# An attention block: the low part of the value projection is made on GpSimd from an fp32 copy instead of on VectorE from PSUM

## The chip, the cores and the metric

One core of one Trainium2 chip runs the whole kernel in one launch. The metric is device time in microseconds (us) of that core. One execution was profiled; the others were only timed.

## The reference

```python
x_n = _group_norm(x, gn_w, gn_b)            # x: 4 images of 256 channels, 32 x 32 pixels
q = _conv1x1(x_n, wq, bq)                   # 256 x 256 matrices applied to every pixel
k = _conv1x1(x_n, wk, bk)
v = _conv1x1(x_n, wv, bv)
q, k, v = (to_heads(q), to_heads(k), to_heads(v))      # 4 heads of 64 channels, 1024 pixels
attn = softmax(einsum('bhqd,bhkd->bhqk', q, k) * 64 ** -0.5)
out = _conv1x1(einsum('bhqk,bhkd->bhqd', attn, v), wp, bp)
return x + out
```

Everything is fp32 in the reference.

## The kernel before, in words

Products run on TensorE in fp16 with each factor split in two: the high part is the fp32 value rounded to fp16, the low part is the rest. A product is then three matmuls, high by high, high by low and low by high. So each tensor that a matmul reads has a high and a low tile, and somebody has to make them.

The work is cut into 128 slots, 32 to an image (`TOTAL`, `SLOTS`); G is the slot's number, g its number within the image, U = G // 4 is a unit (a head and half of its queries, 8 to an image), and each slot takes two blocks of 128 keys. Every engine has its own program, an in-order list of what it does slot by slot, written by hand in a function `slot(G)`; semaphores join them.

What happens in slot G:

- TensorE, in this order: the scores of slot G (`scores`, L707 and L708, into PSUM banks `st[G % 2]`); up to two matmuls for the row maxima of a later unit (L652 for one row tile, L678 for a pair of heads); in odd slots the second half of a projection job (L587); the weighing of slot G - 4 (`weigh`, 24 matmuls, L730 to L733, into `pv`), which needs the exponentials of slot G - 4, their low part and the values' low part; a tiny matmul for group statistics in some slots (L635); in even slots the first half of a new projection job.
- ScalarE: the exponentials of slot G twice, as fp16 `p_hi` (L900) and as fp32 `p` (L908, in place in `st` for even G); in odd slots the eviction of the job that has just ended (`job`, L859 to L879); for the next image, the normalised input (L927, L933).
- VectorE: in even slots `low(...)` (L1004) if a value job ended; in odd slots the low part of the exponentials of the even slot before (`p_low`, L1014, in two halves); the row maxima (L990 for a pair, L985 for one), the normalisation of a finished unit (L1021, L1022), statistics of a later image.
- GpSimd: in even slots the split of a key or query job (`high`, L1216, and `low_kq`, L426), the low part of the exponentials of the odd slot before (`p_low`, L1242); residual additions, the split of outputs (L1230, L1232), the low part of the normalised input (L412), and `about_group_mean` (L403 to L407) and `norm_factors` (L1195 to L1203), the small steps from group statistics to the factors of the next image's normalisation.
- SyncE issues nearly all DMAs, in order, among them the row shift that the first scores of a unit need (L467).

A projection job is `(kind, i, j, image)`, with i the half of the channels and j the half of the pixels; its bank is `gen`, one PSUM bank for all. `JOBS` places it: value jobs start at g = 8, 14, 24 and 30 (in the first image also at 2, and one before slot 0), 16 in all. A value job at G is ended by TensorE in slot G + 1, evicted by ScalarE in slot G + 1 and given its low part in slot G + 2. The next job may use `gen` when `bank_empty` says so.

One pair of row maxima in each even slot is put in the scores bank `st[1]`, which the scores of the next, odd slot need. So `scores(G)` in odd slots waits until VectorE has reduced that pair (`in_scores_bank`, `pair_in_bank`, L700).

The lines that make a value tile before:

```python
# ScalarE, L870: high part straight from PSUM
nc.scalar.activation(v_rows(v_hi, i, j), bank..., ACT.Copy, scale=...).then_inc(s_hi["v"], 1)
# VectorE, L1004: low part = scale * PSUM - high part
nc.vector.scalar_tensor_tensor(out=v_rows(v_lo, i, j), in0=gen..., scalar=..., in1=v_rows(v_hi, i, j), ...)
```

`v_rows` is 8 rows of 64 fp16 numbers with a step of 65 in `v_hi` and of 64 in `v_lo`.

The first image has a table of its own for statistics, `FIRST_STATS = {4: ("mean", 1), 6: ("var", 1)}`: in slot 4 GpSimd ends its list with `about_group_mean`, whose result `dev2` TensorE multiplies in slot 6, right behind the weighing of slot 2 (L635). For the later images these are slots 27 and 31.

Of the kernel before, what the change touches and what calls it, by code (L numbers as in the profile page):

```python
# [7 lines left out]
ALU = mybir.AluOpType  # L8
ACT = mybir.ActivationFunctionType
# [3 lines left out]
def attention_block(nc, x, gn_w, gn_b, wq, bq, wk, bk, wv, bv, wp, bp, out):  # L13
    B, C, IH, IW = x.shape
    HW = IH * IW
    P = 128
# [65 lines left out]
    with ctx:  # L82
        def sb(name, shape, dt=F32):
            return ctx.enter_context(nc.sbuf_tensor(name, shape, dt))

        def sem(name):
            return ctx.enter_context(nc.semaphore(name))
# [33 lines left out]
        z_lo = sb("z_lo", [P, 2, CT, HW], F16)  # L121

        e32 = {n: sb(f"e32_{n}", [P, 2, HALF]) for n in "kq"}
        kq_hi = {n: sb(f"st_hi_{n}", [P, HW], F16) for n in "kq"}
        kq_lo = {n: sb(f"st_lo_{n}", [P, HW], F16) for n in "kq"}

# [68 lines left out]
        s_z0_lo = sem("s_z0_lo")  # L195

        s_gen_full = sem("s_gen_full")
        s_e32 = {n: sem(f"s_e32_{n}") for n in "kq"}
        s_first_hi = {n: sem(f"s_first_hi_{n}") for n in "kq"}
        s_hi = {n: sem(f"s_hi_{n}") for n in "kqv"}  # L200
        s_lo = {n: sem(f"s_lo_{n}") for n in "kqv"}
# [37 lines left out]
        def wait(eng, s, v):  # L239
            if v > 0:  # L240
                eng.wait_ge(s, v)
# [30 lines left out]
        def nth(i, j, b):  # L272
            return 4 * b + 2 * i + j

        def slot_of(G):
            return G if 0 <= G < TOTAL else None
# [83 lines left out]
        def lo_on_dve(G):  # L360
            return in_place(G) or G >= TOTAL - TAIL
# [17 lines left out]
        def quarters(n):  # L379

            return slice(HALF + n * 2 * P, HALF + (n + 1) * 2 * P)

        def halves(j):
            return slice(j * HALF, (j + 1) * HALF)
# [5 lines left out]
        def v_rows(tile, i, j):  # L390
            return tile[:, i, 4 * j:4 * j + 4, :, 0:D].rearrange("p c h d -> p (c h) d")
# [173 lines left out]
        def _(pe):  # L565
# [3 lines left out]
            def bank_empty():  # L569

                if not held:
                    return
                kind, i, j, b = held.pop()
                if kind in "kq":
                    wait(pe, s_e32[kind], nth(i, j, b) + 1)
                elif kind == "v":
                    wait(pe, s_lo[kind], nth(i, j, b) + 1)
                elif kind == "y":
                    wait(pe, s_y, 4 * b + i + 2 * j + 1)
                else:  # L580
                    wait(pe, {"mean": s_gmean, "var": s_gvar}[kind], b + 1)
# [263 lines left out]
        def _(act):  # L845
# [13 lines left out]
            def job(kind, i, j, b, bank=gen):  # L859
                bank_full()  # L860
                if kind in "kq":
                    wait(act, s_lo[kind], nth(i, j, b) - 1)
                    if (i, b) == (0, 0):
                        nc.scalar.activation(kq_hi[kind][:, halves(j)], bank[:, :], ACT.Identity,
                                             bias=bias_s[kind][:, i:i + 1], scale=QKV_SCALE / (Z_SCALE * W_SCALE))\
                          .then_inc(s_first_hi[kind], 1)
                    nc.scalar.activation(e32[kind][:, j, :], bank[:, :], ACT.Identity, bias=bias_s[kind][:, i:i + 1],  # L867
                                         scale=QKV_SCALE / (Z_SCALE * W_SCALE)).then_inc(s_e32[kind], 1)
                if kind == "v":
                    nc.scalar.activation(v_rows(v_hi, i, j), bank[:, :].rearrange("p (n d) -> p n d", d=D), ACT.Copy,  # L870
                                         scale=QKV_SCALE / (Z_SCALE * W_SCALE)).then_inc(s_hi["v"], 1)
                if kind == "y":
                    wait(act, s_out, 64 * b)
                    wait(act, s_bias_y, 1)
                    nc.scalar.activation(y32[:, i, halves(j)], bank[:, :], ACT.Identity,
                                         bias=bias_y[:, i:i + 1], scale=1.0 / (O_SCALE * W_SCALE)).then_inc(s_y, 1)
                if kind == "var":
                    nc.scalar.activation(veps[:, :], bank[:, 0:CT], ACT.Identity, bias=eps[:, 0:1])\
                      .then_inc(s_gvar, 1)  # L879
# [96 lines left out]
        def _(dve):  # L976
# [21 lines left out]
                nc.vector.reduce_max(mx4[:, U // 2 % 2, heads, :], mx8[:, U // 2 % 2, heads, :, :], AX.X)\  # L998
                  .then_inc(s_join, 1)

            def low(kind, i, j, b):

                wait(dve, s_hi[kind], nth(i, j, b) + 1)
                nc.vector.scalar_tensor_tensor(out=v_rows(v_lo, i, j), in0=gen[:, :].rearrange("p (n d) -> p n d", d=D),  # L1004
                                               scalar=QKV_SCALE / (Z_SCALE * W_SCALE), in1=v_rows(v_hi, i, j),
                                               op0=ALU.mult, op1=ALU.subtract).then_inc(s_lo[kind], 1)

            def p_low(G):

                wait(dve, s_exp, G + 1)  # L1010
# [54 lines left out]
            def slot(G):  # L1065
                b, g = place(G)
                tops, olds = reduced_at(G), weighed_at(G)
                todo = job_at(G - 2) if G % 2 == 0 else None
                if todo and todo[0] == "v":
                    low(*todo)  # L1070
                if slot_of(G - 1) is not None and lo_on_dve(G - 1):
                    p_low(G - 1)
                for item in tops[:1]:
                    row_max(*item)
                if stat_at(G):
                    statistic_full(*stat_at(G))
                for old in olds:
                    if old % SPU == SPU - 1:
                        normalise(old // SPU)
                if stat_at(G):  # L1080
                    statistic(*stat_at(G))
                if g in (20, 22, 24, 26) and b + 2 < B:
                    channel_stats(b + 2, (g - 20) // 4, ((g - 20) // 2 % 2,))
                for item in tops[1:]:
                    row_max(*item)
                for U in complete_at(G):
                    join_max(U)
                if G in (1, 2):
                    channel_stats(1, 1, (G - 1,))
# [76 lines left out]
            split_weights(3)  # L1166
            for j in range(2):
                row_max("one", 1, j)
            low("v", 0, 0, 0)
            for j in range(2, 4):  # L1170
                row_max("one", 1, j)
            channel_stats(1, 0)
# [14 lines left out]
        def _(pool):  # L1187
# [17 lines left out]
            def high(kind, i, j, b):  # L1205
# [9 lines left out]
                        wait(pool, s_mx_full, all_full("two", gone))  # L1215
                nc.gpsimd.tensor_copy(kq_hi[kind][:, halves(j)], e32[kind][:, j, :]).then_inc(s_hi[kind], 1)  # L1216

            def residual(i, j, b):
                wait(pool, s_y, 4 * b + i + 2 * j + 1)
                wait(pool, s_xres, 16 * (b + 1))  # L1220
                nc.gpsimd.tensor_tensor(y32[:, i, halves(j)], y32[:, i, halves(j)], xres[:, i, halves(j)], ALU.add)\
                  .then_inc(s_yx, 1)
# [22 lines left out]
            def slot(G):  # L1245
                b, g = place(G)
                todo = job_at(G - 2) if G % 2 == 0 else None
                if todo and todo[0] in "kq":
                    high(*todo)
                    low_kq(pool, *todo)  # L1250
                if slot_of(G - 1) is not None and not lo_on_dve(G - 1):
                    p_low(G - 1)
                if G == 1:
# [39 lines left out]
            low_kq(pool, "q", 0, 0, 0)  # L1293
            low_kq(pool, "k", 0, 1, 0)
            low_kq(pool, "q", 0, 1, 0)
            for G in range(TOTAL):
                slot(G)
            for i in range(CT):
# [25 lines left out]
```

## Time and profile before

| | us |
|---|---|
| median of 3 runs | 379.27 (378.57 to 379.49) |
| the profiled execution | 378.99 |
| its span, first to last instruction | 377.0 |
| TensorE / ScalarE / VectorE / GpSimd busy | 349.6 / 305.8 / 290.8 / 257.4 |

The granted TensorE clock was 1.000 over the span, that is the full 2.4 GHz. 2.0 us of the profiled execution lie outside its span. Busy times are unions over the span; the end of a TensorE matmul is modelled, and a matmul of 512 columns is shown as 0.38 us although the next one starts 0.22 us after it.

### The profile page before, as it was taken

How to read it: one execution, taken by the hardware profiler on the slowest of the kernel's cores; microseconds unless marked ns; L12 is line 12 of the kernel's file. 1: busy time of each engine (PE TensorE's matmuls, PEld its weight loads, DVE VectorE, ACT ScalarE, POOL GpSimd, SP SyncE). 2: the span in 40 equal slices, each digit the busy share in tenths (PEclk: the TensorE clock that was granted, in tenths of full speed). 3: DMA queues.
4: the chain of work that ended last, by engine and by line, in shares of the span. 5: the costliest groups of instructions: out<-in, count | busy, mean ns of one | idle time of the engine just before them, and what ended most of it. 6: DMA issues, size and time to landing. Idle time of an engine off the chain costs nothing.

```text
span 377.0 us, 11185 instructions
## 1 busy us (share of the span) xinstructions
PE 349.6 (93%) x4581; PEld 209.5 (56%) x4581; DVE 290.8 (77%) x443; ACT 305.8 (81%) x379; POOL 257.4 (68%) x227
## 2 busy tenths in 40 slices
PE   0999987999899999999999999999999999989796
PEld 0744554555556556655656456655656556555474
DVE  4789888878797678778887678687878778686375
ACT  1758787888777998988878898988879887887883
POOL 5044974688758797958859798858959495846722
PEclk9999999999999999999999999999999999999999
DMA  6045250141642431061552432021461432060113
GB/s 211 17 129 147 44 118 12 15 145 24 127 144 57 98 73 59 2 195 43 109 163 43 90 80 73 2 85 42 98 172 38 111 69 71 2 197 2 30 30 113
DMA packets 38730, 30.92 MB, mean 82 GB/s; under 512 B 23820, under 2 KB 31512, under 8 KB 38680
## 3 DMA queue, kind: packets, MB, share of 16 engines
q1 hardware_dynamic: 37936, 29.15, 30.7%
q10 hardware_dynamic: 744, 1.06, 0.8%
q8 instruction: 37, 0.61, 0.7%
q14 instruction: 13, 0.11, 0.1%
HBM read 9.44 MB, written 4.19 MB: 36 GB/s over the span
## 4 chain that ended last, share of the span: by engine, by line
PE 54%; ACT 12%; DVE 9%; issue 8%; DMA 6%; POOL 5%; SPq 3%; POOLq 1%; DVEq 1%; ACTq 0%
PE gen L587 11%; PE st L707 10%; PE st L708 9%; PE pv L730 5%; DMA q_max<-shift 5%; ACT p L908 5%; PE pv L733 5%; PE pv L732 4%; ACT p_hi L900 4%; DVE mx L990 4%; PE st L678 3%; PE mx L678 2%; POOL p_lo L1242 2%; DVE v_lo L1004 2%; DVE mx L985 1%
## 5 line engine op out<-in xcount | busy, mean ns | idle before, releaser
L900 ACT ACTIVATE p_hi<-st 128x1024 f16<-128x1024 f32 x127 | 130.4, 1027 | 47.2 <-PE st L708 46.4
L1242 POOL TENSOR_TENSOR p_lo<-p,p_hi 128x1024 f16<-128x1024 f32 x62 | 132.0, 2130 | 39.9 <-ACT p L908 39.3
L730 PEld LDWEIGHTS pv<-v_hi,p_hi 128*128 128x128 f16 x1024 | 93.4, 97 | 28.1 <-issue 14.6
L730 PE MATMUL pv<-v_hi,p_hi 128*128 128x65 f16 x1024 | 106.4, 195 | 0.1
L732 PE MATMUL pv<-v_lo,p_hi 128*128 128x64 f16 x1024 | 105.9, 193 | 0.0
L733 PE MATMUL pv<-v_hi,p_lo 128*128 128x65 f16 x1024 | 105.8, 194 | 0.0
L1014 DVE TENSOR_TENSOR p_lo<-st,p_hi 128x512 f16<-128x512 f32 x126 | 80.9, 684 | 30.9 <-ACT st L908 30.2
L707 PE MATMUL st<-q_twice,k_both 128*128 128x512 f16 x256 | 97.1, 379 | 8.0 <-DMA q_max<-shift 5.2
L732 PEld LDWEIGHTS pv<-v_lo,p_hi 128*128 128x128 f16 x1024 | 93.8, 98 | 6.4
L708 PE MATMUL st<-q_max,k_one 65*128 65x512 f16 x256 | 97.2, 380 | 0.0
L733 PEld LDWEIGHTS pv<-v_hi,p_lo 128*128 128x128 f16 x1024 | 93.9, 97 | 0.0
L990 DVE TENSOR_REDUCE mx<-st 128x2 f32<-128x1024 f32 x52 | 63.7, 1224 | 26.5 <-PE st L678 26.3
L990 DVE TENSOR_REDUCE mx<-mx 128x2 f32<-128x1024 f32 x60 | 73.1, 1218 | 2.4 <-PE mx L678 2.4
L908 ACT ACTIVATE st<-st 128x1024 f32<-128x1024 f32 x63 | 65.4, 1038 | 0.0
L908 ACT ACTIVATE p<-st 128x1024 f32<-128x1024 f32 x64 | 65.2, 1018 | 0.0
L707 PEld LDWEIGHTS st<-q_twice,k_both 128*128 128x128 f16 x256 | 25.4, 99 | 36.5 <-issue 8.0
L708 PEld LDWEIGHTS st<-q_max,k_one 65*128 65x128 f16 x256 | 24.9, 97 | 17.5
L426 POOL TENSOR_TENSOR st_lo_k<-e_k,st_hi_k 128x512 f16<-128x512 f32 x16 | 18.5, 1154 | 10.5 <-ACT e_k L867 8.5
L985 DVE TENSOR_REDUCE mx<-mx 128x1 f32<-128x512 f32 x32 | 21.1, 686 | 4.0 <-PE mx L788 2.1
L587 PE MATMUL gen<-w_hi_v,z_hi 128*128 128x128 f16 x128 | 23.1, 219 | 0.0
L587 PE MATMUL gen<-w_hi_v,z_lo 128*128 128x128 f16 x128 | 23.0, 219 | 0.0
L587 PE MATMUL gen<-w_lo_v,z_hi 128*128 128x128 f16 x128 | 23.0, 219 | 0.0
(183 smaller groups left out, 526.8 us busy)
## 6 DMA issues: line engine op xcount, KB each, us to landing
q_twice<-st_hi_q SPq DMA_DIRECT2D x64, 64.0 KB, 2.3
xres<-in_x_dram SPq DMA_DIRECT2D x4, 1024.0 KB, 5.2
out_dram<-y SPq DMA_DIRECT2D x13, 256.0 KB, 2.3
xin<-in_x_dram SPq DMA_DIRECT2D x6, 512.0 KB, 4.6
k_both<-st_hi_k SPq DMA_DIRECT2D x16, 128.0 KB, 2.3
k_one<-st_hi_k SPq DMA_DIRECT2D x16, 128.0 KB, 2.5
q_max<-st_lo_q SPq DMA_DIRECT2D x32, 64.0 KB, 2.1
k_both<-st_lo_k SPq DMA_DIRECT2D x16, 128.0 KB, 2.3
```

Source lines behind the costliest of these rows:

```text
L587: last = nc.tensor.matmul(dst, a, c, start=first and t == 0 and n == 0, stop=t == CT - 1 and n == 2, skip_group_check=True)
L707: nc.tensor.matmul(dst, k_both[:, head, k], q_twice[:, head, q], start=True, stop=False)
L708: last = nc.tensor.matmul(dst, k_one[:, head, k], q_max[:, head, q], start=False, stop=True)
L730: nc.tensor.matmul(pv_v[:, q, :], hi, vh, start=k == 0 and q == 0, stop=False, skip_group_check=True)
L732: nc.tensor.matmul(pv_v[:, q, 0:D], hi, vl, start=False, stop=False, skip_group_check=True)
L733: last = nc.tensor.matmul(pv_v[:, q, :], lo, vh, start=False, stop=k == NK - 1, skip_group_check=True)
L900: nc.scalar.activation(p_hi[:, G % PR, :, :], scores, ACT.Exp, scale=SM_SCALE / M_SCALE)
L908: nc.scalar.activation(p_full(G), scores, ACT.Exp, scale=SM_SCALE / M_SCALE).then_inc(s_exp, 1)
L985: nc.vector.reduce_max(mx8[:, n // 2 % 2, n % 2, tile, part:part + 1], mxb[j % 2], AX.X)\
L990: nc.vector.reduce_max(mx8[:, n % 2, :, tile, part], bank[:, :].rearrange("p (h k) -> p h k", h=2), AX.X).then_inc(s_mx_free, 1)
L1014: nc.vector.tensor_tensor(p_lo[:, G % PR, c, :], p_full(G)[:, c, :], p_hi[:, G % PR, c, :], ALU.subtract).then_inc(s_plo_dve, 1)
L1242: nc.gpsimd.tensor_tensor(p_lo[:, G % PR, :, :], p_full(G), p_hi[:, G % PR, :, :], ALU.subtract)\
```

## The change

ScalarE evicts the value job once as fp32 into a new tile `e32_v`, and that frees the bank `gen`. GpSimd makes the high part by a copy from `e32_v` and the low part by a subtraction, at the head of its slot G + 2, where it splits keys and queries too. VectorE's `low` is gone. ScalarE's eviction now waits until GpSimd has read `e32_v` of the job before; GpSimd's copy waits until the last weighing that reads the old values is over; TensorE's `weigh` waits for the low part as before, but it comes from GpSimd.

```diff
+        e32_v = sb("e32_v", [P, HALF])
...
+        def last_weighing(i, j, b):
+            return b * SLOTS + (4 * i + 3) * SPU + 2 * j + 1
...
-                if kind in "kq":
+                if kind in "kqv":
                     wait(pe, s_e32[kind], nth(i, j, b) + 1)
-                elif kind == "v":
-                    wait(pe, s_lo[kind], nth(i, j, b) + 1)
...
                 if kind == "v":
-                    nc.scalar.activation(v_rows(v_hi, i, j), bank[:, :].rearrange("p (n d) -> p n d", d=D), ACT.Copy,
-                                         scale=QKV_SCALE / (Z_SCALE * W_SCALE)).then_inc(s_hi["v"], 1)
+                    wait(act, s_lo["v"], nth(i, j, b))
+                    nc.scalar.activation(e32_v[:, :], bank[:, :], ACT.Copy,
+                                         scale=QKV_SCALE / (Z_SCALE * W_SCALE)).then_inc(s_e32["v"], 1)
...
-            def low(kind, i, j, b):
-                wait(dve, s_hi[kind], nth(i, j, b) + 1)
-                nc.vector.scalar_tensor_tensor(out=v_rows(v_lo, i, j), in0=gen[:, :].rearrange("p (n d) -> p n d", d=D),
-                                               scalar=QKV_SCALE / (Z_SCALE * W_SCALE), in1=v_rows(v_hi, i, j),
-                                               op0=ALU.mult, op1=ALU.subtract).then_inc(s_lo[kind], 1)
...
-                todo = job_at(G - 2) if G % 2 == 0 else None      # VectorE, head of slot(G)
-                if todo and todo[0] == "v":
-                    low(*todo)
...
-            low("v", 0, 0, 0)                                     # VectorE, before slot 0
...
+            def split_values(i, j, b):
+                n = nth(i, j, b)
+                full = e32_v[:, :].rearrange("p (n d) -> p n d", d=D)
+                wait(pool, s_e32["v"], n + 1)
+                if n > 3:
+                    wait(pool, s_pv, last_weighing(i, j, b - 1) + 1)
+                nc.gpsimd.tensor_copy(v_rows(v_hi, i, j), full).then_inc(s_hi["v"], 1)
+                wait(pool, s_hi["v"], n + 1)
+                nc.gpsimd.tensor_tensor(v_rows(v_lo, i, j), full, v_rows(v_hi, i, j), ALU.subtract)\
+                  .then_inc(s_lo["v"], 1)
...
                 if todo and todo[0] in "kq":                      # GpSimd, head of slot(G)
                     high(*todo)
                     low_kq(pool, *todo)
+                if todo and todo[0] == "v":
+                    split_values(*todo[1:])
                 if slot_of(G - 1) is not None and not lo_on_dve(G - 1):
                     p_low(G - 1)
...
             low_kq(pool, "q", 0, 1, 0)                            # GpSimd, before slot 0
+            split_values(0, 0, 0)
```

## Rows read from the trace of the kernel before

**Rows 1.** The page: busy time by engine, and the chain that ended last.

```profile
PE 349.6 (93%) x4581; PEld 209.5 (56%) x4581; DVE 290.8 (77%) x443; ACT 305.8 (81%) x379; POOL 257.4 (68%) x227
...
PE gen L587 11%; PE st L707 10%; PE st L708 9%; PE pv L730 5%; DMA q_max<-shift 5%; ACT p L908 5%; PE pv L733 5%; PE pv L732 4%; ACT p_hi L900 4%; DVE mx L990 4%; PE st L678 3%; PE mx L678 2%; POOL p_lo L1242 2%; DVE v_lo L1004 2%; DVE mx L985 1%
```

**Rows 2.** Who waited for whom: us in total, times, longest.

```profile
ACT p_hi L900 <- PE st L708: 46.4, 61, 1.7
...
ACT xin L927 <- POOL z_b L1203: 2.7, 2, 1.3
...
PE st L707 <- DVE mx L990: 1.7, 9, 0.4
```

**Rows 3.** Timeline of VectorE, g = 10 of image 1: start, us, instruction [idle before].

```profile
146.10 0.69 DVE L1004 SCALAR_TENSOR_TENSOR v_lo<-gen,v_hi 128x512 f16<-128x512 f32 x1 [0.84 <-ACT v_hi L870]
146.71 1.22 DVE L990 TENSOR_REDUCE mx<-st 128x2 f32<-128x1024 f32 x1
```

**Rows 4.** Timeline of ScalarE, the same slot and the next.

```profile
145.46 0.61 ACT L870 ACTIVATE v_hi<-gen 128x512 f16<-128x512 f32 x1
...
149.14 1.02 ACT L900 ACTIVATE p_hi<-st 128x1024 f16<-128x1024 f32 x1 [0.71 <-PE st L708]
```

**Rows 5.** Timeline of TensorE, the same slot and the next; g = 17 of image 3.

```profile
145.81 0.41 PE L678 MATMUL st<-st_hi_k,st_hi_q 64*128 64x512 f16 x2
...
147.54 0.38 PE L587 MATMUL gen<-oT_hi,w_lo_p 128*128 128x512 f16 x1
148.07 0.38 PE L707 MATMUL st<-q_twice,k_both 128*128 128x512 f16 x1 [0.16 <-DVE mx L990]
...
334.26 0.38 PE L707 MATMUL st<-q_twice,k_both 128*128 128x512 f16 x1 [0.36 <-DVE mx L990]
```

**Rows 6.** Groups of ScalarE by line and shape: busy, mean ns, idle before.

```profile
L870 ACT ACTIVATE v_hi<-gen 128x512 f16<-128x512 f32 x16 | 9.7, 607 | 0.2 <-PE gen L587 0.2
...
L867 ACT ACTIVATE e_q<-st,bias_s_q 128x512 f32<-128x512 f32 x2 | 1.4, 680 | 0.0
```

**Rows 7.** Groups of GpSimd and of VectorE by line and shape.

```profile
L426 POOL TENSOR_TENSOR st_lo_k<-e_k,st_hi_k 128x512 f16<-128x512 f32 x16 | 18.5, 1154 | 10.5 <-ACT e_k L867 8.5
...
L1216 POOL CAST st_hi_k<-e_k 128x512 f16<-128x512 f32 x14 | 8.5, 609 | 16.1 <-ACT e_k L867 13.8 <-SPq L551 2.2
```

```profile
L1004 DVE SCALAR_TENSOR_TENSOR v_lo<-gen,v_hi 128x512 f16<-128x512 f32 x16 | 11.0, 690 | 5.3 <-ACT v_hi L870 5.0
```

**Rows 8.** Timeline of GpSimd: a key job's split, and the turn of the image.

```profile
109.68 0.61 POOL L1216 CAST st_hi_k<-e_k 128x512 f16<-128x512 f32 x1
...
111.55 2.12 POOL L1242 TENSOR_TENSOR p_lo<-p,p_hi 128x1024 f16<-128x1024 f32 x1
...
122.39 2.13 POOL L1242 TENSOR_TENSOR p_lo<-p,p_hi 128x1024 f16<-128x1024 f32 x1
125.75 0.61 POOL L1216 CAST st_hi_k<-e_k 128x512 f16<-128x512 f32 x1 [1.22 <-ACT e_k L867]
```

**Rows 9.** Timeline of GpSimd in the first image.

```profile
39.20 4.22 POOL L1242 TENSOR_TENSOR p_lo<-p,p_hi 128x1024 f16<-128x1024 f32 x2
...
44.05 0.19 POOL L407 TENSOR_TENSOR dev<-dev,mv 128x2 f32<-128x2 f32 x1
...
63.88 2.13 POOL L1242 TENSOR_TENSOR p_lo<-p,p_hi 128x1024 f16<-128x1024 f32 x1 [5.61 <-ACT p L908]
```

**Rows 10.** Timeline of TensorE in the first image, and at the image's turn.

```profile
44.48 0.19 PE L730 MATMUL pv<-v_hi,p_hi 128*128 128x65 f16 x1
...
45.20 0.36 PE L635 MATMUL pv<-dev,group_avg 128*128 128x2 f32 x2
...
50.77 0.38 PE L652 MATMUL mx<-k_both,q_twice 128*128 128x512 f16 x1
52.03 0.41 PE L678 MATMUL mx<-st_hi_k,st_hi_q 64*128 64x512 f16 x2 [0.88 <-DVE mx L985]
...
128.62 0.19 PE L730 MATMUL pv<-v_hi,p_hi 128*128 128x65 f16 x1
```

More of the change, by code:

```diff
@@ L197, in attention_block @@
         s_gen_full = sem("s_gen_full")
-        s_e32 = {n: sem(f"s_e32_{n}") for n in "kq"}
+        s_e32 = {n: sem(f"s_e32_{n}") for n in "kqv"}
         s_first_hi = {n: sem(f"s_first_hi_{n}") for n in "kq"}
```

## The prediction

> **What bounds the kernel now.** I read the page first. TensorE is busy for 93% of the span, and the chain that ended last runs mostly through its lines; VectorE's `v_lo` line, which the change removes, holds 2% of that chain [rows 1]. That 2% is no gain in itself: the chain goes through whatever came last, and the next latest may be just behind. So I read the waits next. ScalarE waits 46.4 us for scores, so as a rule TensorE sets the pace and ScalarE follows [rows 2]. No row has TensorE waiting for `v_lo`: neither the bank `gen` nor the weighing is held up by it, and freeing `gen` earlier is worth nothing. But TensorE waits nine times for a row maximum that VectorE reduces, 1.7 us together [rows 2], and the question is what stood ahead of that maximum on VectorE. Third I laid the timelines of three engines side by side at one of the nine.
>
> At g = 10 of image 1 VectorE is idle for 0.84 us until ScalarE's `v_hi` ends, makes `v_lo` from 146.10, and only then, at 146.71, reduces the pair in the scores bank, until 147.93 [rows 3]. TensorE had written that pair at 145.81 to 146.22. Its last matmul before the scores of slot 43 starts at 147.54, the scores at 148.07 [rows 5]. A 512-column matmul is followed by the next after 0.22 us (the note under the table of times), so the scores could have started at 147.76: 0.31 us are lost. The wait view gives 0.16 of it, since it counts from the modelled end. Eight of the nine have a wait of 0.16 or 0.17 and a `v_lo` right ahead of the maximum: at g = 17 and 27 of image 0, 11 and 27 of image 1, 11 and 27 of image 2, 1 and 11 of image 3. The ninth is at 334.26 with 0.36 [rows 5] (8 x 0.165 + 0.36 is the 1.7); there the pair itself was written late, behind another wait of TensorE, and `v_lo` had ended before it.
>
> **What is removed.** Sixteen `v_lo` of 690 ns, 11.0 us of VectorE [rows 7]. Nearly all of it was beside other work. Where it stood in the path: without it the maximum at g = 10 can start as the pair is written, some 0.4 us before 146.71, and end by about 147.5. It then needs 0.14 us to reach TensorE (147.93 to 148.07 now [rows 3, 5]), 147.65, just ahead of the 147.76 at which TensorE comes. So each of the eight stalls goes whole: 8 x 0.31 = 2.5 us. What follows a stall moves with it: ScalarE is idle for 0.71 us before the exponentials of slot 43 [rows 4], so it can start them 0.31 us earlier. The other eight `v_lo` give nothing: at those places TensorE waits for something else or for nothing.
>
> **What is kept with another form.** ScalarE's eviction writes 512 fp32 instead of 512 fp16: 607 ns before; the nearest fp32 eviction takes 680 ns but adds a bias [rows 6]. I take 607, since it stays the same copy with a scale. At the upper end 16 x 0.07 = 1.2 us of ScalarE, behind which it has idle time as above: nothing on the path. Its new wait is for the value job before, six slots back or more (three at the start), and GpSimd is long done with that.
>
> **What is added.** Sixteen pairs of a copy and a subtraction on GpSimd. The key job's pair has the same sizes and dtypes: 609 and 1154 ns [rows 7], and from the start of the copy to the start of what follows 111.55 - 109.68 = 1.87 us [rows 8]. I take 1.87. No row shows GpSimd with an output or input in rows of 64 with a step of 65. Below I put the bound at the pair's bare 1.76; above, at a copy as slow as the subtraction, 1.15, and a subtraction as slow as the one of twice the size, 2.12 [rows 8], 3.4 us with the step between them. Nearer the key pair, since a run of 64 contiguous numbers is most of the way to 512.
> The Trainium skill (Perfetto Trace Analysis, on the GpSimd engine instruction) says that GpSimd durations in a profile are unreliable and that the spacing of starts is to be used. Here the durations sum to 1.76 us and the spacing is 1.87 us; by the durations the loss worked out below would be 0.1 us smaller.
>
> Who queues behind the pair on GpSimd: the low exponentials of the odd slot before, which `weigh` needs four slots on. That work has slack. The tightest place is the turn of the image (g = 0), where GpSimd comes late from `norm_factors`: its `p_lo` runs from 122.39 to 124.52 [rows 8] and TensorE takes it up at 128.62 [rows 10], 4.1 us later; 1.87 of it goes, 2.2 us stay. Next there GpSimd is idle for 1.22 us before the key job [rows 8], so that slips by 0.65 us and its consumers are slots away. ScalarE's two waits for `z_b`, 2.7 us [rows 2], stay: `norm_factors` stands ahead of the new pair. At g = 26 the pair fits into GpSimd's idle time ahead of the statistics.
>
> One place has no slack: the first image, slots 4 to 6. There the pair of value job (0, 1) goes between the two `p_lo` that are one row at 39.20 now [rows 9], the second of which is followed by `about_group_mean`, whose `dev2` ends at 44.05 + 0.19 = 44.24 [rows 9]. GpSimd is busy without a break there, so all moves by 1.87: `dev2` ends at 46.11. TensorE multiplies it at 45.20 [rows 10], right behind the weighing of slot 2, and with 0.14 us of signal it comes at 46.25: a new stall of 1.05 us. (In general the pair's length less 0.82.) `v_lo` itself is there at 43.2, before the weighing of slot 2 at 44.48 [rows 10]. Behind TensorE's stall are the maxima, the second half of a query job and all scores after. From 45.20 to 50.77 TensorE has no gap, and at 52.03 it waits for a maximum [rows 10] that VectorE could only start once TensorE's matmul of 50.77 had run; so that wait moves along, and the 1.05 us are carried on. GpSimd's own delay ends in its idle 5.61 us before 63.88 [rows 9], which takes up the pair of slot 10 too. SyncE's queue passes on the key and query copies of that stretch 1.9 us later, ahead of the next row shift, not behind it.
>
> **The sum,** against the profiled execution: 378.99 - 2.5 + 1.05 = 377.5 us. The median of the runs is 0.28 above the profiled one: 377.8 us.
>
> **The rivals.**
> - The early stall isn't there, because GpSimd gets through slot 4 sooner than the rows say or the first image takes it up in its later waits. For it: that stretch has waits of TensorE for VectorE of up to 0.88 us [rows 10]. Against it: they hang on TensorE's own earlier work. Time: 379.27 - 2.5 = 376.8.
> - The gain is given back. ScalarE is busy for 81% [rows 1], and where its idle time before the exponentials is short, the scores come earlier and nothing else does; or the maximum ends no earlier than 147.76 after all (the margin is 0.1 us). Half the gain: 379.27 - 1.25 + 1.05 = 379.1; none: 380.3.
> - Slower: GpSimd becomes what is waited for, through a pair X much longer than 1.87 us, by the step of 65. The price is X - 0.82 in slot 6 of the first image, and at two turns of the image X - 4.0 beyond the slack. With the gain of 2.5 it is slower by over 0.3% (1.14 us) from X = 4.1 on; at X = 5.0 it costs 4.2 + 2.0 - 2.5 = 3.7: 383.0. Against it: X would be more than twice the key pair.
> The Trainium skill (GPSIMD Engine Reference, Engine selection) says to keep elementwise work on VectorE, as GpSimd is about twice as slow for two inputs. The rows give 1154 against 690 ns, 1.7 times; by the page's factor the subtraction would take 1.38 us (an estimate) and the early stall 1.3 us, so the rule speaks for the loss but doesn't turn the sign.
>
> **How the numbers follow.** Forecast 0.50; no early stall 0.12; gain given back in half or whole 0.28; GpSimd the bound 0.10. This kernel's runs tell 0.3%, 1.14 us, from nothing: faster is below 378.1, slower above 380.4. The forecast's own range is 377.2 to 378.6 (a pair of up to 2.4 us, a stall or two kept), of which 0.05 lies in "same". Faster 0.45 + 0.12 = 0.57; same 0.05 + 0.28 = 0.33; slower 0.10. The range goes from below the second case, 376.5, to near the whole loss of the gain, 380.0.
>
> **What would show it.** After: no wait of TensorE's scores for VectorE's maximum but the one near 333; a wait of about 1 us before the statistics matmul of slot 6; pairs on GpSimd 1.9 us apart from what follows; `p_lo` of GpSimd done 2 us before its weighing at the image's turn. Wrong it would be if the eight stalls stay under another name (ScalarE's exponentials, a DMA), if the copy takes over 1.2 us, or if TensorE waits for GpSimd in the later images.

## The result, and the profile after

The changed kernel takes 376.77 us in the median (374.94 to 377.86, 6 runs) where the kernel before takes 378.99 beside it (378.57 to 379.57, 6 runs): ratio 0.9935, 95% interval 0.9908 to 0.9961. The profiled execution took 376.80 us, with a span of 375.0 against 377.0. So it is 2.2 us faster by the medians (the ratio on record goes by the means: 376.57 to 379.05). Forecast was 377.8, with 377.2 to 378.6 as the forecast's own range: the direction is right, and the time lies 0.4 us below that range, though within the wide one (376.5 to 380.0).

The page and the waits after (who waits for whom: us in total, times, longest), to be read against [rows 1] and [rows 2]:

```profile
PE 347.5 (93%) x4581; PEld 209.2 (56%) x4581; DVE 280.6 (75%) x427; ACT 305.6 (82%) x379; POOL 284.0 (76%) x259
```

```profile
ACT p_hi L904 <- PE st L711: 45.2, 61, 1.7
...
PE st L710 <- DMA q_max<-shift: 5.6, 6, 1.8
...
ACT xin L931 <- POOL z_b L1196: 2.9, 3, 1.2
...
PE st L710 <- DVE mx L994: 0.4, 1, 0.4
```

VectorE has 10.2 us less to do, GpSimd 26.6 us more, and ScalarE still waits for scores. What matters is the last line: nine waits of the scores for VectorE's maximum have become one, 0.36 us ahead of the scores at 332.25, which was ahead of those at 334.26 [rows 5].

The slot of [rows 3 to 5], g = 10 of image 1, on VectorE, ScalarE and TensorE, after:

```profile
145.14 1.23 DVE L994 TENSOR_REDUCE mx<-st 128x2 f32<-128x1024 f32 x1 [0.99 <-PE st L681]
146.82 1.29 DVE L1011 TENSOR_TENSOR p_lo<-st,p_hi 128x512 f16<-128x512 f32 x2 [0.45 <-ACT st L912]
```

```profile
147.71 1.02 ACT L904 ACTIVATE p_hi<-st 128x1024 f16<-128x1024 f32 x1 [0.39 <-PE st L711]
```

```profile
144.69 0.41 PE L681 MATMUL st<-st_hi_k,st_hi_q 64*128 64x512 f16 x2
...
146.42 0.38 PE L590 MATMUL gen<-oT_hi,w_lo_p 128*128 128x512 f16 x1
146.64 0.38 PE L710 MATMUL st<-q_twice,k_both 128*128 128x512 f16 x1
```

The maximum starts 0.45 us after the start of the matmul that writes the pair (144.69) instead of 0.90, and ends at 146.37. The scores follow the matmul ahead of them after 0.22 us; before it was 0.53 (147.54 to 148.07 [rows 5]). ScalarE's idle time ahead of the exponentials falls from 0.71 to 0.39.

To see where time went over the whole kernel I took the start of `p_hi` in each slot, after less before: how far the later kernel is behind at that point (minus: ahead). It changes in steps: -0.39 at slot 0 and -0.13 at slot 2 (the start of the kernel, which differs from one execution to the next); +0.52 at slot 7; **-0.31 to -0.34 at each of slots 17, 27, 43, 59, 75, 91, 97 and 107, together -2.6**; -0.17 in two small steps at 33 and 65; and four steps that nothing in the prediction named: -0.38 at 24, +0.48 at 48, +0.48 at 80, +0.18 at 112. They add up to -2.01, the shift of the last exponentials. The four are all at a unit's first slot, whose scores wait for the row shift. They come back below, under the phase experiments.

GpSimd in the first image, its groups by shape, and the turn to image 1, after (compare [rows 7 to 9]):

```profile
38.32 2.13 POOL L1247 TENSOR_TENSOR p_lo<-p,p_hi 128x1024 f16<-128x1024 f32 x1
40.39 0.61 POOL L1218 CAST v_hi<-e_v 128x512 f16<-128x512 f32 x1
41.08 1.12 POOL L1220 TENSOR_TENSOR v_lo<-e_v,v_hi 128x512 f16<-128x512 f32 x1
42.16 2.12 POOL L1247 TENSOR_TENSOR p_lo<-p,p_hi 128x1024 f16<-128x1024 f32 x1
...
44.92 0.20 POOL L412 TENSOR_TENSOR dev<-dev,mv 128x2 f32<-128x2 f32 x1
...
121.11 0.20 POOL L1196 TENSOR_TENSOR z_b<-beta_z,z_m 128x2 f32<-128x2 f32 x1
121.25 0.61 POOL L1218 CAST v_hi<-e_v 128x512 f16<-128x512 f32 x1
...
123.02 2.13 POOL L1247 TENSOR_TENSOR p_lo<-p,p_hi 128x1024 f16<-128x1024 f32 x1
```

```profile
L1220 POOL TENSOR_TENSOR v_lo<-e_v,v_hi 128x512 f16<-128x512 f32 x16 | 17.9, 1119 | 1.3
...
L1218 POOL CAST v_hi<-e_v 128x512 f16<-128x512 f32 x16 | 9.8, 612 | 16.4 <-ACT e_v L874 16.4
```

```profile
45.17 0.38 PE L638 MATMUL pv<-dev,group_avg 128*128 128x2 f32 x2 [0.34 <-POOL dev L412]
```

From the start of the pair to the start of what follows is 42.16 - 40.39 = 1.77 us. `dev2` ends at 45.12 and the statistics matmul of slot 6 waits for it: the new stall is there. At the turn the `p_lo` that is needed four slots on starts 0.63 us later than before (123.02 against 122.39). It ends at 125.15, its weighing starts at 127.50, and nobody waits for it.

### The profile page after: what moved, and what is told of

It reads as the page before. It is cut to its first block, busy times and chain, and to the rows that moved or that the text cites. A ratio compares the mean times of both kernels' runs of the same rounds, so it can differ in the third digit from the quotient of the medians.

```text
span 375.0 us, 11228 instructions
## 1 busy us (share of the span) xinstructions
PE 347.5 (93%) x4581; PEld 209.2 (56%) x4581; DVE 280.6 (75%) x427; ACT 305.6 (82%) x379; POOL 284.0 (76%) x259
## 4 chain that ended last, share of the span: by engine, by line
PE 66%; ACT 7%; DMA 6%; DVE 5%; POOL 5%; issue 5%; SPq 3%; POOLq 2%; DVEq 0%; ACTq 0%
PE gen L590 14%; PE st L710 11%; PE st L711 11%; PE pv L733 7%; PE pv L736 6%; PE pv L735 6%; DMA q_max<-shift 5%; PE st L681 4%; PE mx L681 3%; ACT p_hi L904 3%; ACT p L912 2%; DVE mx L994 2%; POOL p_lo L1247 2%; PE st L590 2%; DVE mx L989 1%
## 5 line engine op out<-in xcount | busy, mean ns | idle before, releaser
L1226 POOL TENSOR_TENSOR y<-y,xres 128x512 f32<-128x512 f32 x14 | 17.7, 1269 | 7.6 <-ACT y L879 7.6
```

## The experiments

Each ratio is to runs of the kernel before on the same chip beside it. The median of those was 379.65 us for e1 to e4, 377.92 for e5 to e8 and 379.32 for e9 to e12, so ratios are to be compared, not times. The ratios on record lie within 0.0004 of those of the means, not on those of the medians, so a difference in us is worked out from two ratios. "Shift" is the start of `p_hi` against the changed kernel's first profile, slot by slot.

**e1_after.** The changed kernel unaltered.

> The changed kernel as it is, beside the kernel before and the other three of this call. Each theory has it 1.5 to 2.5 us faster than before (ratio 0.994 to 0.996). Its trace shows again no wait of the scores for a row maximum at the eight places, a wait for dev2 before the statistics matmul of slot 6, and row-shift transfers at the image's middle whose times differ from those of the first profile, if they hang on what else is under way on the DMA engines.

Measured: 376.72 us, ratio 0.9938 (0.9914 to 0.9961). The same eight stalls are gone. The early one is longer, in the view of TensorE:

```profile
45.02 0.38 PE L638 MATMUL pv<-dev,group_avg 128*128 128x2 f32 x2 [0.65 <-POOL dev L412]
```

It counts 0.81 us by the spacing of starts, against 0.50 in the first profile. That length depends on how TensorE and GpSimd happen to stand to each other; the part on the prediction works it out for seven profiles, in three of which (e7, e8, e9) the stall isn't there at all. The steps at the row shift differ too between these two executions of one kernel: +0.42 at 24, -0.29 at 48, -0.22 at 80, +0.22 at 112.

**e2_dve_filler.** Is it VectorE's place ahead of the maximum, or the bank that is free sooner?

```diff
+ def as_long_as_low(i, j, b):
+     wait(dve, s_e32["v"], nth(i, j, b) + 1)
+     nc.vector.reduce_max(idle_max[:, :], w_in["p"][...], AX.X)      # 128x512 fp32, result unused
  def slot(G):                                                        # VectorE
+     if todo and todo[0] == "v": as_long_as_low(*todo[1:])
```

> VectorE gets back, at the head of the slots where v_lo stood and behind the same kind of wait, an instruction of about 690 ns whose result nobody reads (a maximum over 512 numbers of a weight tile); the bank, GpSimd's pair and ScalarE's eviction stay as changed. If the gain is VectorE's place ahead of the maximum: all eight stalls of 0.3 us are back and the kernel is 2.5 us slower than the changed one (about as fast as before or up to 1 us slower). If the gain came from the bank gen being freed earlier: no difference to the changed one (under 0.5 us).

Measured: 379.53 us, ratio 1.0006 (0.9982 to 1.003). VectorE and TensorE at g = 10 of image 1:

```profile
145.74 0.69 DVE L1065 TENSOR_REDUCE idle_max<-w_in_p 128x1 f32<-128x512 f32 x1 [0.84 <-ACT e_v L875]
146.34 1.22 DVE L995 TENSOR_REDUCE mx<-st 128x2 f32<-128x1024 f32 x1
...
147.71 0.38 PE L711 MATMUL st<-q_twice,k_both 128*128 128x512 f16 x1 [0.15 <-DVE mx L995]
```

This is the picture of [rows 3] and [rows 5] again, and the shift has steps of +0.31 to +0.32 at each of the eight slots. `gen` is still free at ScalarE's eviction here, so the earlier bank is worth nothing that these runs can tell (the interval is 0.9 us either way), and the gain is what stood on VectorE ahead of the maximum.

**e9_filler_behind.** The same reduction, at the end of the slot, behind the maxima. It asks whether VectorE's load costs wherever it stands.

```diff
  def slot(G):                                                        # VectorE
      ...
      for U in complete_at(G): join_max(U)
+     if todo and todo[0] == "v": as_long_as_low(*todo[1:])
```

> The changed kernel with VectorE's extra 690-ns reduction of the earlier run (one operand in SBUF, its result unused), but behind the maxima of the slot instead of ahead of them. VectorE's load is the same as in that run, which gave back the whole 2.5 us. Theory (place): the eight stalls at slots 17, 27, 43, 59, 75, 91, 97 and 107 stay away, and the time is within 0.6 us of the changed kernel, 1.9 to 2.7 us under the kernel before measured beside it. Rival (load): VectorE's 11 us of extra work cost whatever their place, since the next slot's work starts later by 0.69 us in the slots that follow: ScalarE's waits for the join maximum (row maxima) grow, and the time is again within 0.5 us of the kernel before.

Measured: 378.58 us, ratio 0.9987 (0.9968 to 1.0006). The eight stalls stay away, but it isn't within 0.6 us of the changed kernel: (0.9987 - 0.9935) x 379.3 is 2.0 us, so the first theory is half a miss. The shift shows where: +0.2 at slot 12 and +0.4 at 13, +0.21 at 29, +0.35 at 33, +0.21 at 61, +0.35 at 65, together 1.7. Other steps are not the filler's: +0.58 at 24, -0.52 at 80 and -0.46 at 112 are the row shift's, and -0.52 at slot 7 is the early stall, which is missing here although GpSimd's order is the changed kernel's (no wait ahead of the matmul):

```profile
45.12 0.36 PE L639 MATMUL pv<-dev,group_avg 128*128 128x2 f32 x2
```

For slot 29, VectorE:

```profile
105.72 0.63 DVE L1065 TENSOR_REDUCE idle_max<-w_in_p 128x1 f32<-128x512 f32 x1
106.27 1.28 DVE L1012 TENSOR_TENSOR p_lo<-st,p_hi 128x512 f16<-128x512 f32 x2
...
109.18 0.15 DVE L1099 COPY gmean<-pv 128x2 f32<-128x2 f32 x1
```

The next slot's work starts late, and behind it the copy of the group mean, for which TensorE's weighing waits (109.39, 0.53 us after the matmul ahead of it, where the changed kernel has 0.31) and on GpSimd the chain that ends in `z_b`. Both places cost, but different waits: ahead of the maximum 2.5 us at eight slots, behind it 1.7 us at the turns of the image and in the first image.

**e4_dve_both.** ScalarE evicts in fp32 as in the change, but VectorE makes both parts, at the end of its slot.

```diff
+ nc.vector.tensor_copy(v_rows(v_hi, i, j), full).then_inc(s_hi["v"], 1)
+ nc.vector.tensor_tensor(v_rows(v_lo, i, j), full, v_rows(v_hi, i, j), ALU.subtract)...  # both off GpSimd
```

> GpSimd has none of the new work: VectorE makes both parts from the fp32 copy, but at the end of its even slots, behind the row maxima. VectorE then has more work than before (a copy and a subtraction, some 1.2 us for 0.69). If the order ahead of the maximum was the loss and not VectorE's load: 1.5 to 3 us faster than before, no stall at the eight places and no wait for dev2 in slot 6. If it is the load: slower than the kernel before, with the scores or the low exponentials of the next slot late by some 0.3 us or more at the sixteen places.

Measured: 387.09 us, ratio 1.0198 (1.0167 to 1.0229). VectorE's groups, and ScalarE's wait for the factors of the next image:

```profile
L1070 DVE TENSOR_TENSOR v_lo<-e_v,v_hi 128x512 f16<-128x512 f32 x16 | 11.9, 744 | 0.5
L1068 DVE CAST v_hi<-e_v 128x512 f16<-128x512 f32 x16 | 9.3, 580 | 0.0
```

```profile
ACT xin L931 <- POOL z_b L1211: 4.3, 2, 2.1
```

So the second alternative came true, in the main: again none of the eight stalls, but 3.4 us are lost from slot 0 to slot 23, in the first image, with more at the turns. Many of the places are e9's (12, 13, 29, 33, 61, 65), with twice the load (580 + 744 ns). But the profile ends 8.4 us behind the changed kernel's, where e9's ends 1.3 behind, and the steps of +1.2, +0.5, +0.3 and +0.5 at slots 2, 6, 18 and 19 are new; they were not followed further.

**e5_low_behind.** GpSimd makes the high part and VectorE the low one, from SBUF, at the end of its slot.

```diff
- nc.gpsimd.tensor_tensor(v_rows(v_lo, i, j), full, v_rows(v_hi, i, j), ALU.subtract)...
+ nc.vector.tensor_tensor(v_rows(v_lo, i, j), full, v_rows(v_hi, i, j), ALU.subtract)...
```

> ScalarE's fp32 eviction and GpSimd's copy stay, but the subtraction goes back to VectorE, at the end of its slot, behind the row maxima: VectorE has as much work as in the kernel before (some 690 ns, sixteen times), only in another place, and GpSimd 1.1 us less per value job than in the changed kernel. If the place ahead of the maximum is what cost: no stall at the eight places, dev2 in time for slot 6, 0 to 1 us faster than the changed kernel, 2.5 to 3.5 faster than before. If VectorE's load is what cost: as slow as before (within 1 us).

Measured: 393.64 us, ratio 1.04 (1.0363 to 1.0436): every theory missed. VectorE, GpSimd and TensorE at the turn to image 1:

```profile
125.22 2.60 DVE L1065 TENSOR_TENSOR v_lo<-e_v,v_hi 128x512 f16<-128x512 f32 x1 [2.52 <-POOL v_hi L1228]
```

```profile
125.14 2.12 POOL L1254 TENSOR_TENSOR p_lo<-p,p_hi 128x1024 f16<-128x1024 f32 x1
```

```profile
128.47 0.39 PE L710 MATMUL st<-q_twice,k_both 128*128 128x512 f16 x1 [3.10 <-DVE p_lo L1011]
```

Two things come together. VectorE stands still for 2.52 us until GpSimd has gone through `norm_factors` to the value's high part; and its subtraction then takes 2.60 us, beside a GpSimd subtraction, where one of the same shape took 0.68 (the first, at 27.88). The sixteen average 1610 ns. With `gen` in PSUM as one input it was 690 [rows 7]. The Trainium skill (SBUF — State Buffer, "two separate sides") says that a VectorE operation with two inputs in SBUF and a GpSimd operation that reads SBUF exclude each other for their whole length. That fits: GpSimd's 2.12 us end at 127.26 and VectorE's subtraction 0.56 us after that. It also bears on e4, of whose sixteen subtractions one took 1.52 us. A third loss comes behind the pauses of 3.1 us that TensorE makes at the first two turns (the 3.10 above and one like it at 219.43): its granted clock is 0.50 from 129.87 to 133.28 and from 218.61 to 225.44. The shift grows by 1.95 and 2.63 us at slots 34 and 66, and by 2.05 and 2.22 more at 35 and 67; how much of this is the clock's wasn't separated.

**e6_pool_twice.** A second pair on GpSimd with its results thrown away, for the twelve value jobs of images 1 to 3: 3.77 us from the start of the first copy to what follows (120.82 to 124.59), 2.0 more than in the changed kernel.

```diff
+ if n > 3:
+     then(nc.gpsimd.tensor_copy(spare[:, 0, :], e32_v[:, :]))
+     then(nc.gpsimd.tensor_tensor(spare[:, 1, :]..., full, v_rows(v_hi, i, j), ALU.subtract))
```

> GpSimd does a second copy and subtraction into spare tiles for each value job but the first four (twelve times, the pair then some 3.7 us instead of 1.8). By my reckoning of the slack at the image's turn (4.1 us before the change, 2.2 after) the low exponentials still come 0.3 us before their weighing, so no wait of TensorE's weighing for GpSimd, or one of a few tenths, and the time within 0.5 us of the changed kernel. If GpSimd is already near its bound: TensorE waits for p_lo at the turns, by 1 us or more each.

Measured: 379.9 us, ratio 1.0044 (1.0024 to 1.0064), (1.0044 - 0.9935) x 377.9 = 4.1 us above the changed kernel and not within 0.5. The weighing still waits for no `p_lo` (at the turn it ends at 126.72, and the weighing starts at 127.06), so the slack that was worked out for it holds. The loss is elsewhere: the `z_b` chain is late, TensorE's waits for ScalarE at the turns (123.60 and 209.59 here) grow from 0.92 to 1.50 us each, and SyncE's queue is late. The queue of SyncE ahead of slot 72, this kernel and then the changed one:

```profile
218.57 2.52 SPq L462 DMA_DIRECT2D q_twice<-st_hi_q  x4
221.13 1.23 SPq L466 DMA_DIRECT2D q_max<-st_lo_q  x2
222.41 1.24 SPq L473 DMA_DIRECT2D q_max<-shift  x2
```

```profile
217.78 1.24 SPq L461 DMA_DIRECT2D q_twice<-st_hi_q  x2
219.06 1.23 SPq L465 DMA_DIRECT2D q_max<-st_lo_q  x2
221.45 1.15 SPq L472 DMA_DIRECT2D q_max<-shift  x2
```

The copies of the query's parts wait for GpSimd and the row shift waits behind them: it is issued 0.96 us later, and the scores wait 0.87 us for it at 225.09. The profile also has 0.8 us of the lower clock that e10 shows. So the change itself has GpSimd within some 2 us per value job of being the bound.

**e3_mean_first, e12_mean_first_again.** Can the early stall be had back? In slot 4 GpSimd does `about_group_mean` ahead of its `p_lo`.

```diff
+ if G == 4: about_group_mean(pool, 1)
  if slot_of(G - 1) is not None and not lo_on_dve(G - 1): p_low(G - 1)
  ...
- if stat and stat[0] == "mean":
+ if stat and stat[0] == "mean" and G != 4:
```

> In slot 4 of the first image GpSimd does the group mean's three small steps ahead of its low exponentials instead of behind them. If the early stall is GpSimd's lateness with dev2: the wait before the statistics matmul of slot 6 goes, 0.5 us of the profile (0.5 to 1.0 by run), and the kernel is that much faster than the changed one. Rival, that the first image takes the stall up in its later waits: same end, as the maxima near 52 us wait longer by what was gained.

> The changed kernel with the first image's second group mean moved ahead on GpSimd's queue, a second time, now beside its combination with the 64 waits. If the stall at slot 6 is worth its length: 0.5 to 1.0 us under the changed kernel, 2.8 to 3.3 under the kernel before (ratio 0.991 to 0.993). Rival (the gain is taken up later by waits for row-shift transfers): 0.994, as the changed kernel.

Measured: 376.19 us, ratio 0.9918 (0.9888 to 0.9949), and 376.01 us, ratio 0.9914 (0.9893 to 0.9935). GpSimd and TensorE in the second:

```profile
43.56 0.20 POOL L412 TENSOR_TENSOR dev<-dev,mv 128x2 f32<-128x2 f32 x1
43.71 2.13 POOL L1247 TENSOR_TENSOR p_lo<-p,p_hi 128x1024 f16<-128x1024 f32 x1
```

```profile
45.20 0.36 PE L638 MATMUL pv<-dev,group_avg 128*128 128x2 f32 x2
```

The wait is gone and the shift falls by 0.52 at slot 7 in both, which no later slot takes up. Both ratios are below the changed kernel's two by 0.0017 to 0.0024, which is the right size but inside the intervals. That the wait is gone isn't proof by itself either, since three other profiles of the unaltered order lack it. The margin is: here `dev2` ends at 43.76, 1.44 us ahead of its matmul (1.13 in e3), and in those three only 0.2 to 0.3 us ahead. The times alone don't prove the gain.

**e7_phase_64, e8_phase_128, e11_before_64.** What are the steps at slots 24, 48, 80 and 112? The row shift is two copies of 1 KB, which mostly land after 1.9 to 2.0 us, but some take 2.9 to 3.7. The fourteen profiles have 448 such copies, and 49 took 2.9 us or more. Each of the 49 had a transfer of the queue "instruction" (16 KB of program, on one of the DMA engines, 0.9 to 1.4 us long) that began 0.5 to 1.5 us after the copy was issued, and landed 1.05 to 1.53 us after that transfer's end. To move these loads I added instructions that do nothing to TensorE's program:

```diff
  pe.wait_ge(s_const, 2)
+ for _ in range(64): pe.wait_ge(s_const, 1)      # already met; 128 in e8; e11: in the kernel before
```

> TensorE's program gets 64 waits more that are already met, while it waits for its first data, so that nothing is later but every following instruction lies 64 places further on. If the row-shift transfers that land late (2.9 us and more instead of 2.0 to 2.8) do so because the 16 KB transfer that loads instructions is under way on a DMA engine that they use: these loads come some 2.3 us earlier against the slots (at 155.8 instead of 158.1 us at the middle of image 1), the four slow transfers at 93, 157, 242 and 326 us land within 2.8 us, the waits of the scores for them fall by 0.3 to 0.8 us each, and the kernel is 1 to 2.5 us faster than the changed one. If the transposes or stores behind them delay them: no change in their durations.

> The same with 128 waits: the loads come some 4.6 us earlier against the slots, again not at the four transfers. If the loads are the cause: like the 64 waits, 1 to 2.5 us faster than the changed kernel. If not: no change.

> The kernel before with the same 64 waits at the head of TensorE's program. If the loads' places are counted in TensorE's instructions, then here too the late row-shift transfers move to slots 16, 48, 72 and 104 or near them, and those at 24, 80 and 112 go back to 2.0 us; the time moves by what those slots take, between 1 us less and 1 us more, and the eight stalls at slots 17, 27, 43, 59, 75, 91, 97 and 107 stay. If instead the kernel before has its loads placed by the other engines' programs, the late slots stay the ones of its own profile (24 and 80).

Measured: ratios 0.9939 (0.9917 to 0.9962), 1.0004 (0.9984 to 1.0025) and 1.0007 (0.9984 to 1.003). The DMA view of 92.4 to 96.0, around the row shift of slot 24, in the changed kernel, where it is issued at 92.41, and in e7, where it is issued at 92.39:

```profile
q8 instruction: 1, 0.02, 1.5%
issues: line engine op xcount, KB each, median us to landing
q_max<-shift SPq DMA_DIRECT2D x2, 1.0 KB, 2.6
```

```profile
issues: line engine op xcount, KB each, median us to landing
q_max<-shift SPq DMA_DIRECT2D x2, 1.0 KB, 1.9
```

The scores that need it, in the changed kernel and in e7:

```profile
95.95 0.39 PE L710 MATMUL st<-q_twice,k_both 128*128 128x512 f16 x1 [0.71 <-DMA q_max<-shift]
```

```profile
95.06 0.38 PE L710 MATMUL st<-q_twice,k_both 128*128 128x512 f16 x1
```

The load that runs from 93.56 to 94.44 in the changed kernel, under way within the second copy (issued at 92.96, landed at 95.90), is over at 92.84 in e7 (it began at 91.95, ahead of the window shown); the transfer is on time and nobody waits. Instead e7 has waits of 1.1 to 1.4 us (by spacing) at slots 16, 48, 72 and 104; 24, 80 and 112 are clear. In e8 they are at 16, 40, 72, 96 and 104, 0.95 to 1.6 us each; in e11, the kernel before, at 16, 48, 72 and 104, 0.8 to 1.1, with 24 down to 0.29 and 80 and 112 clear. So it is the place of TensorE's program that decides which transfer is hit. What the expectations made of it in time missed: neither e7 nor e8 is 1 to 2.5 us faster than the changed kernel, since other transfers are hit instead. The Trainium skill (Runtime: NRT & Kernel Launch, "Instruction fetch mechanics") says that the sequencer loads the next 16 KB block by its own DMA queue and that the cost is mostly hidden. The traces don't contradict that for TensorE itself: in the changed kernel's profile one wait of its matmuls, of 0.4 us, has no cause that the profile names (its weight loads, which overlap them, have more such waits, so it isn't proven either). What is not hidden is the small transfer that is held up.

The runs say what such a draw is worth: e8 differs from the changed kernel in nothing but 128 idle instructions and is at 1.0004, 2.6 us slower by ratio. Its own profile shows 1.6 of it (a span of 376.6 against 375.0).

**e10_mean_first_64.** The two edits together, as the candidate for the fastest.

> Two edits that each stood a little below or level with the changed kernel, together: the first image's second group mean one value-free slot earlier on GpSimd's queue (removes the stall of 0.5 to 1.05 us at slot 6), and 64 waits already met at the head of TensorE's program (moves the instruction loads). If both gains are real and add up: 0.6 us plus 0.3 to 0.9 us under the changed kernel, 375.2 us where the kernel before gives 379. Rival (the second edit is only another draw of the collisions between instruction loads and row-shift transfers): 376.0, the same as the first alone.

Measured: 376.48 us, ratio 0.9927 (0.9904 to 0.995): not better than the first edit alone. At slot 112 its profile is 1.42 us ahead of the changed kernel's, at slot 123 only 0.56. Between them stands this, on TensorE, and the granted clock (the sixth column after the engines' busy times, 1.00 is full) of three stretches:

```profile
347.32 0.39 PE L710 MATMUL st<-q_twice,k_both 128*128 128x512 f16 x1 [1.78 <-DMA q_max<-shift]
...
350.25 0.64 PE L711 MATMUL st<-q_max,k_one 65*128 65x512 f16 x1
350.67 0.63 PE L710 MATMUL st<-q_twice,k_both 128*128 128x512 f16 x1
```

```profile
340.00:347.00 7.00, 5.17 (x92) 3.51 (x88) 4.39 (x8) 5.89 (x8) 6.92 (x6) 1.00 0.03 3
347.60:350.00 2.40, 2.40 (x29) 1.76 (x28) 0.00 (x0) 1.25 (x2) 2.40 (x2) 0.56 0.31 68
350.00:352.50 2.50, 2.50 (x31) 1.38 (x29) 1.29 (x2) 1.58 (x2) 0.02 (x1) 0.74 0.00 0
```

After a pause of 1.8 us that is in every version, the matmuls run at half pace (0.42 us from start to start instead of 0.22): the clock is granted at its lower level, 1.2 GHz. In the changed kernel's own profile the same pause is there and the clock stays:

```profile
349.00:351.50 2.50, 2.50 (x42) 1.66 (x41) 0.00 (x0) 1.69 (x2) 2.43 (x2) 1.00 0.30 66
```

The timed runs differ in the same way: many have a mean granted clock of 0.995 or less. Those at 0.999 or 1.000 alone give the same order. Their mean is 376.4 us for e1 (7 runs) and 378.7 for e2 (4) where the kernel before has 379.1 (6); 378.2 for e8 (6) where it has 377.8 (15); 377.9 for e9 (3) and 376.1 for e12 (4) where it has 378.9 (11). So neither the gain nor e2's loss of it is the clock's.

The fastest version by ratio is then the changed kernel with the mean first, 0.9914 to 0.9918, about 0.7 us under the changed kernel if its stall is taken at its length.

## Why the prediction was right

- **The eight stalls.** Right in number, place and size: 8 x 0.31 = 2.5 was forecast, 2.6 measured; the ninth stayed. e2 brings them back by one VectorE instruction ahead of the maximum and nothing else, and e9, with the same instruction behind it, doesn't. The reason given holds: the waits were for what stood ahead of the maximum, and the 2% of `v_lo` in the chain was no measure.
- **"Nearly all of it was beside other work"** is right for where it stood. But the sentence says less than it seems: e9 shows that the same 690 ns behind the maxima cost 1.7 us at other waits. A load is not free because its present place isn't waited for.
- **The GpSimd pair.** 1.87 us was taken, 1.77 measured; the rows of 64 with a step of 65 cost nothing (612 ns for the copy against 609 [rows 7], 1119 against 1154 for the subtraction).
- **The early stall.** Where it is there, it is at the matmul named and is carried on. But it was forecast at 1.05 us and measured at 0.50 and 0.81 in the changed kernel's two profiles: the one term that was mis-sized. 0.1 us is the shorter pair. The rest is where GpSimd stands to TensorE: in the first profile its `p_lo` started at 38.32 against 39.20 [rows 9], 0.88 us earlier, while TensorE (by `p_hi` at slots 2 to 6) was only 0.52 earlier, so 1.05 - 0.10 - 0.88 + 0.52 = 0.59 us were to be expected. Seven profiles have the changed kernel's order on GpSimd up to there. The same sum gives 0.59, 0.90, 0.96 and 0.42 us for the first, e1, e2 and e6, and the steps at slot 7 against the kernel before are 0.52, 0.84, 0.89 and 0.36. For e7, e8 and e9 it gives -0.05 to -0.18, and there is no stall. So the path is right, and its length is a matter of the execution, from nothing to 0.9 us. The sum took one execution's phase as fixed.
- **GpSimd's slack and ScalarE's `z_b` waits.** Right as forecast: no weighing waits for GpSimd's `p_lo`, not even in e6; at the turn it is done 2.35 us ahead of its weighing, where 2.2 was worked out; and the wait for `z_b` goes from 2.7 to 2.9 us in total. "Ahead of the next row shift, not behind it" was right for this pair and has little margin: e6 breaks it with 2.0 us more.
- **The sum.** 378.99 - 2.6 + 0.5 (the stall) - 0.5 (the start of this execution) + 0.8 (the four row-shift steps: -0.38 + 0.48 + 0.48 + 0.18) - 0.2 (slots 33 and 65) = 377.0, and the profiled execution took 376.8. The terms that the prediction knew give -2.1. Those that it didn't know are of the same size as what it argued about, -0.5, +0.8 and -0.2, and nearly cancel here. The profile was forecast at 377.5 and the median at 377.8; they came 0.7 and 1.0 us lower, the median below the forecast's own range. That the sum came this near is in part luck; the mechanism is not.
- **The rivals.** "No early stall" gives 376.8, which is the median to the hundredth and nearer than the forecast. The stall is in both traces of the changed kernel, but it is shorter than forecast, and e7, e8 and e9 show that an execution can be without it, for the reason that this rival names first: GpSimd gets through slot 4 sooner against TensorE than the rows say. So this rival is half right. "Gain given back" and "GpSimd the bound" are excluded by the eight steps, which stay, by the pair's 1.77 us, and by e6. (By its own prices the last one is slower by 1.14 us from X = 4.15 on, not 4.1.)

What stays open: why the clock falls after the pause near 348 us in some executions and not in others, what costs e4 its first steps, and how large the mean-first gain is beyond the traces.

## What to carry to other kernels

Ask of an instruction what stands right behind it on its own in-order queue and who waits for that: 0.69 us on VectorE cost nothing at eight places, 0.31 at eight others, and other waits when it was put elsewhere. When work goes to a slower engine with slack, list what queues behind it and look for the one place where the queue has no gap; here a small statistics step could be put ahead, and its result was ready 1.1 to 1.4 us before it was needed. And below about 1% of this kernel, compare steps slot by slot before believing a time: a change of program length alone moved it by up to 2.6 us.

## What the runs showed of the hardware that was not expected

- Loads of TensorE's own program (37 of 16 KB in each profile) share the DMA engines with the kernel's transfers. One of them holds up a 1 KB copy on the path by about 1 us (2.6 against 1.9 in the median of two parts, single ones up to 3.7). The hits wander with the length of TensorE's program: slots 24, 48, 80, 112 in one build; 16, 48, 72, 104 with 64 instructions more.
- A VectorE subtraction of 512 columns with both inputs in SBUF took 0.68 us alone and 2.60 beside a GpSimd subtraction; reductions from SBUF and subtractions with one input in PSUM kept their length (0.68 to 0.69 for e2's filler, 0.63 to 0.68 for e9's, 0.68 to 0.69 for the sixteen `v_lo` of the kernel before).
- Six of the fourteen profiles (e2, e3, e4, e6, e7, e10) show the clock of TensorE at its lower level for some 3 us after the same 1.8 us pause, which all fourteen have, at a cost of about 0.8 us (e10: from 1.42 us ahead to 0.56). e5's two pauses of 3.1 us had it both times.
